# Self-loop scores of the edge attention: laid into each loaded score tile by VectorE instead of stored to the score matrix by GpSimd

## The chip, the cores and the metric

One Trainium2 chip, one core. The metric is the device time of one launch in microseconds (us), the median of several runs. The program is a whole two-layer graph network; the change touches one stage of it, the edge attention of layer 0.

## The reference, cut to what matters

The graph has 1250 nodes and 21250 directed edges. The attention adds one loop edge per node, computes a score for each edge and head, and takes a softmax over the edges that end at a node:

```python
loop = jnp.arange(n, dtype=edge_index.dtype)
src = jnp.concatenate([edge_index[0], loop])
dst = jnp.concatenate([edge_index[1], loop])
xl = (x @ Wl).reshape(n, H, D)
xr = (x @ Wr).reshape(n, H, D)
msg = xl[src] + xr[dst]
act = jnp.where(msg > 0, msg, NEG_SLOPE * msg)
e = jnp.einsum('ehd,hd->eh', act, att)
m = jax.ops.segment_max(e, dst, num_segments=n)
p = jnp.exp(e - m[dst])
denom = jax.ops.segment_sum(p, dst, num_segments=n)
alpha = p / (denom[dst] + 1e-16)
out = jax.ops.segment_sum(alpha[..., None] * xl[src], dst, num_segments=n)
out = out.reshape(n, HID)
return out @ W_up
```

H is 4 heads, HID is 256. An edge's score depends on its two nodes alone, so edges that occur several times share one score and differ only by a count.

## The kernel before, in words

**The score matrix.** The kernel keeps a dense matrix in device memory, `scores` (1250 x 1250 cells of 4 heads, f32, the head innermost). Every cell is first filled with -1e30 (`Fill`). GpSimd then writes the scores of the edges into their cells. The counts of the edges lie in a second matrix, `at`.

**Self-loop scores.** `front_phase` computes the score of each node with itself, tile by tile (10 tiles of 125 nodes), into the SBUF tile `loops` [125, 10, 4] (L387, L388). `Edges.diagonal` (L581) stores it to the diagonal of `scores` with eleven GpSimd DMAs (L587, L588), each counting on the semaphore `s_sc`.

**Edge scores.** `Edges` (L516) works through the edges in 84 batches of 2 x 128. For each batch GpSimd gathers rows of `xl` and `xr` (L572), VectorE scores them (`EdgeTurns.step`, L652 to L656), and GpSimd scatters the scores (L579). The order on GpSimd is written out in `Edges.gpsimd` (L597): gathers run five batches ahead, scatters start seven batches behind, and `diagonal` stands in front of the first scatter. A scatter waits for all earlier writes of `s_sc`, the eleven of the diagonal among them. These instructions run beside three stages in turn: the counting stage, the linear attention `mix0` and its output product `out0`. `FirstScores.load` (L632) waits until every score has landed and loads score tile 0 while `out0` still runs.

**The edge attention, `gat_phase` (L1065).** It starts when `out0` has ended, and goes over 10 tiles of 125 target nodes. A score tile is [125, 1250, 4] f32; three of them are held (`DEEP`), and SyncE loads tile t + 3 when tile t has been read. For tile t:
- VectorE takes the maximum per target and head. For tile 0 these are four reductions (`first_maxima`, L1178). For the others it is a tree: `halves` (L1186) folds the tile to one half in a buffer, and `maxima` (L1192, L1196) folds that on and reduces it.
- ScalarE takes the exponentials, head by head (L1284); TensorE transposes them (`spread`, L1340); VectorE multiplies them by the counts (`weigh`, L1217); TensorE multiplies by the node rows (`gather`, L1354).
- VectorE divides by the sum (`quotient`, L1234 to L1239), TensorE turns the result (L1363), ScalarE and VectorE split it into a high and a low part (L1288 and `rest`, L1244), and TensorE multiplies by `W_up` (`product`, L180 to L182).
- The result is added to the residual, normalized and scored for the experts (`GateTile`) one to three tiles later.

The orders are written out by hand, one loop per engine, and the engines meet at semaphores. VectorE's loop at step t has `weigh(t, 0)`, `quotient(t-1)`, `variance(t-2)`, `halves(t+1)`, `rest(t-1)`, `weigh(t, 1)`, `normal(t-2)`, `maxima(t+1)`, `weigh(t, 2)`, `weigh(t, 3)`. TensorE's has `gather(t, 0)`, a part of the expert scores, `spread(t, 2)`, `product(t-1, 0)`, 16 matmuls whose result nobody reads (`idle`, L1379), `gather(t, 1)`, `spread(t, 3)`, `product(t-1, 1)`, 10 more such matmuls, `gather(t, 2)`, `spread(t+1, 0)`, `gather(t, 3)`, `spread(t+1, 1)`, `turn_result(t)`. `Link` is a helper that makes VectorE wait for the end of its own last instruction; instructions without it follow each other with a small overlap.

Of the kernel before, what the change touches and what calls it, by code (L numbers as in the profile page):

```python
# [5 lines left out]
F32 = mybir.dt.float32  # L6
# [509 lines left out]
class Edges:  # L516
# [6 lines left out]
    def __init__(self, ph, src, dst, att, xl, xr, scores, loops, ring):  # L523
        self.src, self.dst, self.att, self.xl, self.xr = src, dst, att, xl, xr
        self.scores, self.loops, self.fill = scores, loops, None
# [48 lines left out]
    def scatter(self, pool, b, j):  # L574
        if j == 0:
            pool.wait_ge(self.s_e, b + 1)
        k = EB * b + j
        pool.wait_ge(self.s_sc, 16 * (T + 1) + 16 * k)
        pool.indirect_dma_start(self.scores, self.at(2, k), self.e[:, k, :], None).then_inc(self.s_sc, 16)  # L579

    def diagonal(self, pool):  # L581
        pool.wait_ge(self.fill.s_fill, self.fill.count)
        flat = self.scores.rearrange("s h -> (s h)")
        diag = flat[0:(N * N - 1) * HEADS].rearrange("(i x) -> i x", x=(N + 1) * HEADS)
        for t in range(T):
            n = min(R, N - 1 - t * R)
            pool.dma_start(diag[t * R:t * R + n, 0:HEADS], self.loops[0:n, t, :]).then_inc(self.s_sc, 16)  # L587
        pool.dma_start(self.scores[N * N - 1:N * N, :], self.loops[R - 1:R, T - 1, :]).then_inc(self.s_sc, 16)  # L588
# [5 lines left out]
    def landed(self, eng):  # L594
        eng.wait_ge(self.s_sc, 16 * (T + 1) + 16 * ET)

    def gpsimd(self, pool, first, end):  # L597
# [5 lines left out]
        for b in range(first, end):  # L603
            done = range(self.written(b - 1) if b else 0, self.written(b))
            if 0 in done:
                self.diagonal(pool)
# [458 lines left out]
def gat_phase(nc, first, scores, at, xl, ident, w_up, bias, part, dst, normed, gate_w, prob_out):  # L1065

    with Phase(nc, "gat") as ph:
# [7 lines left out]
        inv = ph.sb("inv", [R, 2, HEADS], F32)  # L1075
        res = ph.sb("res", [R, 2, HID], F32)
# [24 lines left out]
        with nc.Block(no_gpsimd_drain=True) as block:  # L1101
# [69 lines left out]
            def _(dve):  # L1171
                tree = Link(dve, s_tree)
                level = rows_x[:, :, :].rearrange("p t c -> p (t c)")[:, 0:N // 2 * HEADS].rearrange("p (s h) -> p s h", h=HEADS)

                def first_maxima():
                    dve.wait_ge(s_sc[0], LANDED)
                    for a in range(HEADS):
                        dve.tensor_reduce(top[:, 0, a:a + 1], sc[0][:, :, a], AX.X, ALU.max, negate=True).then_inc(s_top, 1)  # L1178

                def halves(t):  # L1180
# [3 lines left out]
                    if t == 1:  # L1184
                        dve.wait_ge(s_one, 1 + T)
                    tree(dve.tensor_tensor(level[:, :, :], sc[h][:, 0:N // 2, :], sc[h][:, N // 2:N, :], ALU.max))  # L1186
# [2673 lines left out]
def gps_kernel(nc, x, src, dst, rms_w, w_down, wl, wr, att, w_up, wq, bq, wk, bk, wv, bv, wo, bo,  # L3860
# [13 lines left out]
    with Phase(nc, "all") as keep:  # L3874
# [8 lines left out]
        with Phase(nc, "ffn0") as ffn0:  # L3883
            chosen = ffn0.sb("chosen", [CAPR, LIST, E_N], I32)
            share = ffn0.sb("share", [CAPR, LIST, E_N], F32)
            prob = ffn0.sb("prob", [R, T, E_N], F32)
            scored = Phase(nc, "scored")
            first = FirstScores(scored, scores)
            with Phase(nc, "layer0") as layer:
                act = activations(layer)  # L3890
                loops = layer.sb("loops", [R, T, HEADS], F32)
                with Phase(nc, "edge") as edge:
                    edges = Edges(edge, src, dst, att, xl, xr, scores, loops, first.ring)
# [85 lines left out]
```

## Time and profile before

| | us |
|---|---|
| median of 3 runs | 2928.65 |
| lowest and highest | 2922.87, 2935.39 |
| the profiled execution, its own time | 2933.26 |
| its span | 2931.5 |
| mean granted TensorE clock, share of full | 0.948 |

The span is the time from the first to the last instruction in the profile; the profiled execution's own time lies 1.8 us above it. Engines are written PE (TensorE), PEld (its weight loads), DVE (VectorE), ACT (ScalarE), POOL (GpSimd), SPq (SyncE's queue of DMAs).

### The profile page before, as it was taken

What the parts mean: (1) busy time and instruction counts of PE and PEld (TensorE: products, weight loads), DVE (VectorE), ACT (ScalarE), POOL (GpSimd) and SP (SyncE); (2) the same over time, 40 slices, a digit from 0 to 9 for tenths busy, and PEclk for the clock granted to TensorE, in tenths of its full rate; (3) what the DMA queues carried; (4) which work ended last, traced back from release to release, by engine and by line L of the source; (5) the groups of instructions that cost most, each with busy time, mean ns of one, the idle gap of its engine ahead of it and who ended that gap; (6) DMA issues with size and microseconds to landing.
All of it is one profiled execution on the core that took longest, in us unless ns stands there. A gap on an engine that the chain in (4) does not pass through costs nothing. (4 is left out here: it accounts for less than half of the span.)

```text
span 2931.5 us, 51143 instructions
## 1 busy us (share of the span) xinstructions
PE 2658.5 (91%) x19410; PEld 2503.5 (85%) x19410; DVE 1606.4 (55%) x3217; ACT 958.8 (33%) x1921; POOL 794.4 (27%) x772
## 2 busy tenths in 40 slices
PE   6677899999885998699979999899998999999788
PEld 6545899999885997588869999899998999999577
DVE  7777687777625886655553222354546332225755
ACT  4566433333203553244431010233334120001243
POOL 0567767667630342122200000000000001100054
PEclk9888999999995998799989999999999999999899
DMA  8834433433749873478753101111212653224382
GB/s 250 279 114 116 116 105 100 116 95 88 215 111 219 202 199 107 110 185 213 189 128 96 46 30 53 33 58 31 62 31 100 184 157 89 65 62 121 123 281 75
DMA packets 202067, 362.90 MB, mean 124 GB/s; under 512 B 33654, under 2 KB 135246, under 8 KB 200595
## 3 DMA queue, kind: packets, MB, share of 16 engines
q1 hardware_dynamic: 164193, 277.59, 32.3%
q0 software_dynamic: 36112, 80.96, 10.9%
q8 instruction: 150, 2.46, 0.4%
q10 hardware_dynamic: 1540, 1.30, 0.2%
q14 instruction: 72, 0.59, 0.1%
HBM read 272.97 MB, written 98.15 MB: 127 GB/s over the span
## 5 line engine op out<-in xcount | busy, mean ns | idle before, releaser
L180 PE MATMUL mix_bank<-sums_w_hi,layer_act_hi 128*125 128x256 f32 x1280 | 360.1, 281 | 0.0
L181 PE MATMUL mix_bank<-sums_w_lo,layer_act_hi 128*125 128x256 f32 x1280 | 359.2, 281 | 0.0
L182 PE MATMUL mix_bank<-sums_w_hi,layer_act_lo 128*125 128x256 f32 x1280 | 358.8, 280 | 0.0
L3195 POOL TENSOR_TENSOR sage_add<-sage_add,sage_bias 125x256 f32<-125x256 f32 x40 | 29.4, 736 | 1194.3 <-DMA sage_add<-resid 1194.3
L180 PEld LDWEIGHTS mix_bank<-sums_w_hi,layer_act_hi 128*125 128x125 f32 x1280 | 237.7, 186 | 0.8
L181 PEld LDWEIGHTS mix_bank<-sums_w_lo,layer_act_hi 128*125 128x125 f32 x1280 | 237.8, 186 | 0.2
L182 PEld LDWEIGHTS mix_bank<-sums_w_hi,layer_act_lo 128*125 128x125 f32 x1280 | 237.9, 186 | 0.0
L579 POOL DMA_INDIRECT scores<-edge_e,edge_idx x168 | 180.8, 1076 | 132.7 <-DMA scores<-edge_e,edge_idx 91.1
L572 POOL DMA_INDIRECT scored_ring<-xl,edge_idx x168 | 173.6, 1033 | 150.4 <-issue 129.5
L572 POOL DMA_INDIRECT scored_ring<-xr,edge_idx x168 | 170.8, 1017 | 51.5 <-issue 50.0
L929 PE MATMUL count_pa<-count_hot_s,count_hot_d 125*125 125x416 bf16 (+1 forms) x624 | 137.5, 383 | 26.5 <-DVE count_hot_s L839 24.6
L929 PEld LDWEIGHTS count_pa<-count_hot_s,count_hot_d 125*125 125x125 bf16 x624 | 94.0, 156 | 70.5 <-DVE count_hot_s L839 37.5
L180 PE MATMUL mix_bank<-layer_act_hi,mix_wq_hi 128*128 128x416 f32 (+1 forms) x384 | 137.5, 358 | 14.8 <-DVE mix_wq_lo L1612 14.7
L839 DVE TENSOR_SCALAR count_hot_s<-targets_node,targets_ends 125x1250 bf16<-125x1250 f16 x208 | 112.0, 574 | 53.9 <-issue 31.4
L182 PE MATMUL mix_bank<-layer_act_hi,mix_wq_lo 128*128 128x416 f32 (+1 forms) x384 | 136.1, 354 | 0.0
L181 PE MATMUL mix_bank<-layer_act_lo,mix_wq_hi 128*128 128x416 f32 (+1 forms) x384 | 135.7, 353 | 0.0
L1607 DVE SCALAR_TENSOR_TENSOR sums_y<-mix_bank,mix_ex 125x128 f32<-125x128 f32 (+2 forms) x104 | 37.3, 358 | 178.6 <-ACT mix_ex L1728 178.3
L3207 DVE TENSOR_TENSOR sage_z_lo<-sage_pz,sage_z_hi 125x256 fp32r<-125x256 f32 x80 | 33.9, 424 | 168.8 <-ACT sage_z_hi L3307 168.8
L1644 DVE RECIPROCAL sums_num<-sums_num 128x416 f32<-128x416 f32 (+1 forms) x42 | 115.8, 2758 | 19.0 <-ACT sums_num L1754 17.8
L1354 PE MATMUL gat_po<-gat_vals,gat_wgt 125*125 125x66 f32 x800 | 103.4, 290 | 15.2 <-DVE gat_wgt L1217 9.6
L1354 PEld LDWEIGHTS gat_po<-gat_vals,gat_wgt 125*125 125x125 f32 x800 | 100.7, 207 | 16.2 <-DVE gat_wgt L1217 10.2
L3267 DVE SCALAR_TENSOR_TENSOR sage_own<-sage_pagg,all_deg_inv,sage_own 125x256 f32<-125x256 f32 x70 | 33.8, 483 | 136.7 <-PE sage_pagg L3411 130.9
(630 smaller groups left out, 8554.9 us busy)
## 6 DMA issues: line engine op xcount, KB each, us to landing
ffn_raw<-in_L_ffn_w_dram SPq DMA_DIRECT2D x16, 2048.0 KB, 13.0
scores<-targets_hole SPq DMA_DIRECT2D x40, 546.9 KB
ffn_raw<-in_L_ffn_W_dram SPq DMA_DIRECT2D x16, 1024.0 KB
gat_sc<-scores SPq DMA_DIRECT2D x6, 2187.5 KB
lasting_raw<-in_L_mix_w_qkv_dram SPq DMA_DIRECT2D x24, 512.0 KB, 3.9
scored_ring<-scores SPq DMA_DIRECT2D x4, 2187.5 KB
layer_slab<-in_L_gnn_W_neigh_dram SPq DMA_DIRECT2D x7, 1024.0 KB
layer_slab<-in_L_gnn_W_self_dram SPq DMA_DIRECT2D x7, 1024.0 KB
```

Of the source, the lines that this page charges most:

```text
L180: pe.matmul(out, lhs[0], rhs[0], start=first, stop=False)
L181: pe.matmul(out, lhs[0], rhs[1], start=False, stop=False)
L182: return pe.matmul(out, lhs[1], rhs[0], start=False, stop=last)
L572: pool.indirect_dma_start(buf[:, slot, j, :], None, x, self.at(row, EB * b + j)).then_inc(self.s_g[slot], 16)
L579: pool.indirect_dma_start(self.scores, self.at(2, k), self.e[:, k, :], None).then_inc(self.s_sc, 16)
L839: dve.tensor_scalar(hot_s[:, j, :], node[:, :], ends[:, 0, j % 2, bass.ds(q, 1)], None, ALU.is_equal).then_inc(s_hot, 1)
L929: ins = pe.matmul(pa[:, c, 0:n], hot_d[:, j, :], hot_s[:, j, o:o + n], start=False, stop=False)
L1354: ins = pe.matmul(po[:, a * XW:(a + 1) * XW], wgt[:, a, b, :], vals[:, b, a, :], start=b == 0, stop=b == T - 1)
L1607: dve.scalar_tensor_tensor(y[0:p, U % 3, 0:n], from_, more, ex[0:p, U % 2, 0:n], ALU.add, ALU.max).then_inc(s_val, 1)
L1644: dve.reciprocal(num[:, o:o + n], num[:, o:o + n]).then_inc(s_rec, 1)
L3207: dve.tensor_tensor(z[1][:, u % T, :], pz[u % 4][:, 0:SLAB], z[0][:, u % T, :].bitcast(F32), ALU.subtract) \
L3267: dve.scalar_tensor_tensor(total, pagg[u % 2][:, 0:SLAB], deg_inv[:, t:t + 1], own[:, u % 2, :], ALU.mult, ALU.add).then_inc(s_tot, 1)
```

## The change

The eleven DMAs of `diagonal` are gone, and with them their share of the counts that the scatters and `landed` wait for. The first scatter waits for the filling instead. `loops` moves from the layer's buffers to a longer-lived set, so that `gat_phase` can read it. There, `own_edge(t, a)` lays the loop's score of head a into the 125 x 125 block of the loaded tile t that holds the diagonal: each cell becomes the larger of itself and `aside + loops`, where `aside` is 0 on the diagonal and -4e30 elsewhere. It is issued four times for a tile, in front of the four reductions for tile 0 and in front of the fold of `halves` for the others, and a `Link` stands behind the four. `aside` is made once, ahead of tile 0.

```diff
-        pool.wait_ge(self.s_sc, 16 * (T + 1) + 16 * k)
+        if k:
+            pool.wait_ge(self.s_sc, 16 * k)
+        else:
+            pool.wait_ge(self.fill.s_fill, self.fill.count)
         pool.indirect_dma_start(self.scores, self.at(2, k), self.e[:, k, :], None).then_inc(self.s_sc, 16)

-    def diagonal(self, pool):
-        pool.wait_ge(self.fill.s_fill, self.fill.count)
-        flat = self.scores.rearrange("s h -> (s h)")
-        diag = flat[0:(N * N - 1) * HEADS].rearrange("(i x) -> i x", x=(N + 1) * HEADS)
-        for t in range(T):
-            n = min(R, N - 1 - t * R)
-            pool.dma_start(diag[t * R:t * R + n, 0:HEADS], self.loops[0:n, t, :]).then_inc(self.s_sc, 16)
-        pool.dma_start(self.scores[N * N - 1:N * N, :], self.loops[R - 1:R, T - 1, :]).then_inc(self.s_sc, 16)
...
-        eng.wait_ge(self.s_sc, 16 * (T + 1) + 16 * ET)
+        eng.wait_ge(self.s_sc, 16 * ET)
...
-            if 0 in done:
-                self.diagonal(pool)
...
+        aside = ph.sb("aside", [R, R], F32)
...
+                def own_edge(t, a):
+
+                    cells = sc[t % DEEP][:, t * R:(t + 1) * R, a]
+                    return dve.scalar_tensor_tensor(cells, aside[:, :], loops[:, t, a:a + 1], cells, ALU.add, ALU.max)
+
                 def first_maxima():
+                    tree(dve.tensor_scalar(aside[:, :], ident[0:R, 0:R], -1.0, -4.0 * NEG, ALU.add, ALU.mult))
                     dve.wait_ge(s_sc[0], LANDED)
+                    for a in range(HEADS):
+                        ins = own_edge(0, a)
+                    tree(ins)
                     for a in range(HEADS):
                         dve.tensor_reduce(top[:, 0, a:a + 1], sc[0][:, :, a], AX.X, ALU.max, negate=True).then_inc(s_top, 1)
...
                     if t == 1:
                         dve.wait_ge(s_one, 1 + T)
+                    for a in range(HEADS):
+                        ins = own_edge(t, a)
+                    tree(ins)
                     tree(dve.tensor_tensor(level[:, :, :], sc[h][:, 0:N // 2, :], sc[h][:, N // 2:N, :], ALU.max))
```

## Rows read from the trace of the kernel before

**Rows 1.** The page: busy time and share of the span of each engine.
```profile
PE 2658.5 (91%) x19410; PEld 2503.5 (85%) x19410; DVE 1606.4 (55%) x3217; ACT 958.8 (33%) x1921; POOL 794.4 (27%) x772
```
**Rows 2.** Stretches: start:end, length, PE, PEld, DVE, ACT, POOL, PEclk, DMA share, GB/s.
```profile
1009.00:1031.00 22.00, 21.86 (x187) 21.04 (x186) 19.20 (x39) 12.66 (x12) 8.41 (x4) 1.00 0.85 214
```
**Rows 3.** Order of time on POOL: start, duration, instruction, [idle before it <- releaser].
```profile
162.84 5.61 POOL L587 DMA_DIRECT2D scores<-layer_loops  x10
...
172.80 1.23 POOL L572 DMA_INDIRECT scored_ring<-xl,edge_idx  x1 [3.85 <-DVE edge_e L656]
```
**Rows 4.** Order of time where the output product ends and the attention begins.
```profile
871.40 0.97 POOL L579 DMA_INDIRECT scores<-edge_e,edge_idx  x1 [2.31 <-DMA scores<-edge_e,edge_idx]
...
881.47 0.84 SPq L38 DMA_DIRECT2D part<-out_res  x2
...
890.37 9.20 DVE L1178 TENSOR_REDUCE gat_top<-scored_ring 125x1 f32<-125x1250 f32 x4 [8.92 <-PEq L98]
```
**Rows 5.** Order of time in the attention's first three tiles.
```profile
905.77 4.47 PE L1354 MATMUL gat_po<-gat_vals,gat_wgt 125*125 125x66 f32 x20 [5.59 <-POOL gat_vals L1156]
...
917.58 2.76 DVE L1186 TENSOR_TENSOR gat_rows_x<-gat_sc 125x2500 f32<-125x2500 f32 x1 [16.19 <-DMA gat_sc<-scores]
...
922.02 4.47 PE L1354 MATMUL gat_po<-gat_vals,gat_wgt 125*125 125x66 f32 x20 [9.59 <-DVE gat_wgt L1217]
...
943.52 0.42 DVE L1244 TENSOR_TENSOR gat_gat_lo<-gat_pr,gat_gat_hi 128x250 fp32r<-128x250 f32 x1
...
948.09 0.77 PE L180 MATMUL gat_pr<-gat_up_hi,gat_gat_hi 128*125 128x512 f32 x1
```
**Rows 6.** Order of time on PE and DVE in the steady part of the attention.
```profile
969.72 0.50 PE L180 MATMUL gat_pr<-gat_up_hi,gat_gat_hi 128*125 128x512 f32 x1 [0.44 <-DVE gat_gat_lo L1244]
...
1009.05 2.75 DVE L1186 TENSOR_TENSOR gat_rows_x<-gat_sc 125x2500 f32<-125x2500 f32 x1
...
1026.24 2.38 PE L1354 MATMUL gat_po<-gat_vals,gat_wgt 125*125 125x66 f32 x20
...
1028.65 0.23 DVE L1062 TENSOR_REDUCE ffn_prob<-gat_po 125x8 f32<-125x64 f32 x1 [0.56 <-PE gat_po L1354]
...
1030.93 0.15 DVE L1002 TENSOR_SCALAR gat_var<-gat_mv 125x1 f32<-125x1 f32 x1
1031.00 2.75 DVE L1186 TENSOR_TENSOR gat_rows_x<-scored_ring 125x2500 f32<-125x2500 f32 x1
...
1033.79 0.42 DVE L1244 TENSOR_TENSOR gat_gat_lo<-gat_pr,gat_gat_hi 128x250 fp32r<-128x250 f32 x1
...
1034.26 0.50 PE L180 MATMUL gat_pr<-gat_up_hi,gat_gat_hi 128*125 128x512 f32 x1
```
**Rows 7.** Single lines: duration in ns least/median/greatest, first and last start, shapes.
```profile
L1203 DVE TENSOR_TENSOR gat_cnt<-gat_cnt,all_ident x10: 288/290/1647, 899.5 to 1107.7; 125x125 f32<-125x125 f32 x10
L728 DVE TENSOR_REDUCE targets_lim<-targets_rows x1: 409/409/409, 48.4 to 48.4; 85x1 f32<-85x250 f32 x1
L2575 DVE SCALAR_TENSOR_TENSOR choose_within<-choose_far,choose_place x1: 514/514/514, 1195.0 to 1195.0; 125x80 f16<-125x80 f32 x1
L2595 DVE TENSOR_TENSOR ffn_share<-ffn_share,choose_said x1: 204/204/204, 1208.6 to 1208.6; 104x24 f32<-104x24 f32 x1
```
**Rows 8.** Order of time on PE near the attention's end: an instruction behind a pause.
```profile
1138.69 0.43 PE L1363 MATMUL gat_pr<-all_ident,gat_res 125*128 125x125 f32 x2 [1.27 <-DVE gat_res L1239]
```
**Rows 9.** Stretches with or behind three pauses (columns as in rows 2).
```profile
780.00:782.00 2.00, 2.00 (x20) 1.90 (x18) 1.90 (x5) 0.00 (x0) 1.63 (x2) 1.00 0.85 325
...
1138.00:1144.00 6.00, 5.16 (x22) 4.03 (x23) 3.73 (x14) 1.74 (x5) 0.90 (x2) 0.72 0.24 72
...
2004.00:2006.00 2.00, 2.00 (x12) 1.96 (x12) 1.41 (x4) 1.83 (x4) 0.00 (x0) 1.00 0.84 235
```
**Rows 10.** PE's pauses elsewhere, order of time; the last stands for four alike.
```profile
778.61 0.35 PE L180 MATMUL out_bank<-out_w_hi,layer_act_hi 128*125 128x256 f32 x1 [2.17 <-DVE out_res L2114]
...
2003.17 0.43 PE L180 MATMUL mix_bank<-layer_act_hi,mix_wq_hi 128*128 128x418 f32 x1 [1.18 <-DVE mix_wq_lo L1612]
```

More of the change, by code:

```diff
@@ L516, with __init__ @@
 class Edges:
-    def __init__(self, ph, src, dst, att, xl, xr, scores, loops, ring):
+    def __init__(self, ph, src, dst, att, xl, xr, scores, ring):
         self.src, self.dst, self.att, self.xl, self.xr = src, dst, att, xl, xr
-        self.scores, self.loops, self.fill = scores, loops, None
+        self.scores, self.fill = scores, None
         self.idx = ph.sb("idx", [P, 3, ET], I32)
@@ L1062, in keep, with gat_phase @@
         dve.tensor_reduce(self.prob[:, n, :], every, AX.X, ALU.add).then_inc(self.s_prob, 1)
-def gat_phase(nc, first, scores, at, xl, ident, w_up, bias, part, dst, normed, gate_w, prob_out):
+def gat_phase(nc, first, scores, loops, at, xl, ident, w_up, bias, part, dst, normed, gate_w, prob_out):
     with Phase(nc, "gat") as ph:
@@ L3886, in gps_kernel @@
             prob = ffn0.sb("prob", [R, T, E_N], F32)
+            loops = ffn0.sb("loops", [R, T, HEADS], F32)
             scored = Phase(nc, "scored")
@@ L3890, in gps_kernel @@
                 act = activations(layer)
-                loops = layer.sb("loops", [R, T, HEADS], F32)
                 with Phase(nc, "edge") as edge:
-                    edges = Edges(edge, src, dst, att, xl, xr, scores, loops, first.ring)
+                    edges = Edges(edge, src, dst, att, xl, xr, scores, first.ring)
                     begun = MixStart(edge, wq, wk, wv)
@@ L3913, in gps_kernel @@
                     run.__exit__(None, None, None)
-            gat_phase(nc, first, scores, at, xl, ident, w_up, bo, part, xs[0], y[0], gate0_w, prob)
+            gat_phase(nc, first, scores, loops, at, xl, ident, w_up, bo, part, xs[0], y[0], gate0_w, prob)
             ffn0.takes(scored)
```

## The prediction

> **What bounds the kernel now.** I read the page first. Over the whole launch TensorE is busy 91% of the span and VectorE 55% [rows 1], but the change touches only two places, so I read those stage by stage. The stretches come next. In the steady part of the attention TensorE is busy 21.86 of 22 us and VectorE 19.20, at full clock [rows 2]. 21.95 us is also the period of a tile: the fold of one tile starts at 1009.05 and the next at 1031.00 [rows 6]. So TensorE looks like the bound and VectorE seems to have 2.8 us to spare in each tile. That reading has to be tested in the order of time, because part of TensorE's work are the 26 unread matmuls, and because a full engine can still be released by another one.
>
> The order of time of both engines over one period shows the following loop [rows 6]. TensorE's `gather(t, 3)` runs from 1026.24 to 1028.62. VectorE waits for it (idle 0.56 us) and starts the next stretch at 1028.65: quotient, statistics and variance to 1031.08, the fold 1031.00 to 1033.75, `rest` 1033.79 to 1034.21. TensorE's `product` starts at 1034.26, 0.05 us after `rest` has ended. From there TensorE works without a pause to the end of its next `gather(t, 3)`. The loop is closed: 5.6 us on VectorE, then 16.4 us on TensorE, which is the whole period. Inside VectorE's 5.6 us nothing is idle, and TensorE fills that time with work that ends just as `rest` does. Three tiles earlier TensorE even waited 0.44 us for `rest` [rows 6]. So both engines bound the loop at this point, and the fold lies in VectorE's part. The chain of waits on the page follows only the last 3% of the span and says nothing about this stage.
>
> **The part that is removed.** GpSimd issues eleven DMAs for the diagonal, ten of them in 5.61 us from 162.84, and then sits idle for another 3.85 us until VectorE's edge scores release the next gather at 172.80 [rows 3]. Without the eleven it reaches the same wait some 6 us earlier and leaves it at the same time. Gain: 0. The first scatter's new wait, for the filling, costs nothing either, since the diagonal stood behind the same wait and started with no idle time [rows 3]. The later scatters and `landed` only lose eleven counts that were in long before. Even if GpSimd did run earlier, its last scatter is issued at 871.40, while the output product's last store is issued at 881.47 and the attention starts at 890.37, released by the barrier behind TensorE's queue and not by the score tile [rows 4]. 10 us of cover stand between GpSimd and the end of that stage. The 1250 small writes that go were moved when the DMA engines had room. Bounds of this part: 0 to -6 us; I take 0.
>
> **The part that is added: one own_edge.** It is a VectorE instruction on 125 x 125 f32 from SBUF. The nearest unstrided row is the addition of the identity to the counts, same size: 290 ns [rows 7]. But here the cells lie 16 bytes apart, since the head is innermost, for the operand that is read and for the result. What such a step costs is seen in the reductions. The first maxima reduce 1250 cells 16 bytes apart, 9.20 us for four, 2.30 us each [rows 4]; an unstrided reduction of 250 takes 409 ns, of which 250 x 1.04 are elements if they go at the rate of the fold (2.75 us less a start of 0.15, over 2500 elements) [rows 6, 7]. So unstrided 1.04 ns for an element, strided (2300 - 150) / 1250 = 1.72 ns. An addition that reads and writes f32 at 20 to 32 bytes takes 204 ns for 24 elements [rows 7], and less a start of 150 to 160 that is 1.8 to 2.2 ns. Both agree on about 1.9, so one own_edge is 0.155 + 125 x 1.9 = 0.39 us. Lower bound: 0.29. Upper bound: the instruction with f16 results 20 bytes apart, 514 ns for 80 elements or 4.5 ns for each [rows 7], which would make it 0.72 us; I take 0.39, since the f32 row is nearer in type.
>
> The Trainium skill has a rule that speaks against this change (SBUF — State Buffer, the note on cachelines in "Door 1: The DMA port swizzle"): full rate needs at least two accesses in a 16-byte line, and each step to a new line is charged. Every cell here is in a line of its own. This trace agrees, 1.72 against 1.04 ns. By the page on VectorE alone (VectorE: DVE Perf Modes, "Mode 1× (REGULAR) — the baseline"), one element in a cycle whatever the stride, own_edge would stay at 0.29 us, and the sum below would be 8 x 0.96 = 7.7 instead of 10.9 us.
>
> **Four of them and the Link.** Instructions without a Link overlap: the variance ends at 1031.08, the fold has started at 1031.00, so 0.08 us [rows 6]. The four take 4 x (0.39 - 0.08) = 1.24 us. Behind the fourth stands a Link, so the fold, which overlapped the instruction ahead of it by 0.08 before, now starts some 0.04 us after it (as `rest` does after the linked fold, 1033.75 to 1033.79 [rows 6]): 0.12 us more. Sum for a tile: 1.36 us (bounds 4 x 0.21 + 0.12 = 0.96 and 4 x 0.64 + 0.12 = 2.7).
>
> **Which tiles pay.** The folds are those of tiles 1 to 9.
> - Tile 0 (the first maxima, plus `aside`, about 1.7 us): hidden. Its first `weigh` is ready about 901.4, and TensorE starts `gather(0, 0)` at 905.77, released by GpSimd's copy of the rows [rows 5]. VectorE then idles 16.19 us for score tile 1 [rows 5]. If that cover were gone it would cost 1.7 us.
> - Tile 1: pays. The fold starts when the tile lands, 917.58, and the `weigh` behind it releases TensorE at 922.02 [rows 5].
> - Tile 2: hidden. `rest` ends at 943.94, the product it feeds starts at 948.09 because TensorE, at half clock, comes from other work [rows 5]; 4.1 us of cover.
> - Tiles 3 to 9, seven of them: pay in full, by the loop above. VectorE's idle time in a period, the 0.56 us [rows 6] among it, lies outside the 5.6 us, where it waits for TensorE's own work, and shifts with that.
>
> That is 8 x 1.36 = 10.9 us.
>
> **What the new pause may do to the clock.** TensorE will pause 1.36 us in front of `product` in each of seven tiles. Near the attention's end it paused 1.27 us [rows 8], and over the 6 us from 1138 its granted clock was 0.72 of the full 2.4 GHz on average, a part of it at the lower level of 1.2 GHz [rows 9]: 6 x 0.28 = 1.7 us of work lost. But a pause of 2.17 us in the output product and four of 1.18 us in the second `mix` [rows 10] left the clock at 1.00 (the first and one of the four stand in [rows 9]). One pause of six lost the clock, so I charge 7 x 1/6 x 1.7 = 2.0 us (bounds 0 and 12).
>
> **Sum.** 10.9 + 2.0 = 12.9 us. The profiled execution took 2933.26 us (span 2931.5), so 2946.2 us for its like; it lay 4.6 us above the median of the runs, and against that median of 2928.65 I forecast 2941.6 us.
>
> **The rivals.**
> - *VectorE's slack takes it.* It has 2.8 us idle in a period [rows 2] and the change adds 1.36. Then only tile 1 pays, and the time is 2928.65 + 1.4 = 2930, not slower in any measurable way. Against it: the 0.05 us between `rest` and `product` [rows 6]. It would hold if TensorE came to `product` later than `rest` ends by more than 1.36 us.
> - *GpSimd's relief reaches the end.* If the whole chain of scatters moves up by 6 us and the stage's barrier with it, the time is 2928.65 - 6 + 12.9 = 2935.5, and with the slack taking the rest 2924. Against it: the idle 3.85 us and the 10 us of cover [rows 3, 4]. It decides only if the attention's start waits for `landed`.
> - *The clock falls at every pause.* 10.9 + 7 x 1.7 = 22.8 us, 2951.5. For it: the only pause of this length in this very stage did it [rows 8, 9].
> - *Strided writes are dear.* 0.72 us for one own_edge, 2.7 for a tile, 8 x 2.7 = 21.6 plus 2: 2952. For it: one row, of another type [rows 7].
>
> **How the numbers follow.** The forecast has 0.62, the clock rival 0.14, the dear writes 0.10, the slack 0.08, GpSimd's relief 0.04, and 0.02 is left for what I don't see. I take 0.5%, 14.6 us, as what a measurement of this kernel can tell from no change, its own runs spreading over 12.5 us. The forecast's own range is 7.7 to 16 us, so about a fifth of its 0.62 is over the bound; with both dear rivals, slower by over 0.5% gets 0.37. Faster by over 0.5% needs a mechanism that I see only in the two combined: 0.04. The rest, 0.59, is within. The range reaches from below the slack's case to above both dear ones, less the outer tenths: 2929 to 2957.
>
> **What would show it.** In the changed profile: four instructions of own_edge for each tile with 0.39 us each; the fold starting 1.4 us later behind the variance; TensorE's L180 behind a pause of some 1.3 us released by `rest` (L1244) from tile 3 on; a period of 23.3 us against 21.95; GpSimd idle about 10 us in front of the gather at 172.80, and the attention starting at 890 as before. The forecast is wrong if the period stays near 22 us, if the clock falls in the middle of the attention (a period over 24.5), or if the start at 890.37 moves.

## The result and the profile after

| | before | after |
|---|---|---|
| median, us (15 runs each, beside each other) | 2926.27 | 2942.53 |
| lowest and highest | 2922.8, 2937.18 | 2934.51, 2953.0 |
| the profiled execution, its own time | 2933.26 | 2949.02 |
| its span | 2931.5 | 2946.9 |
| mean granted clock, share of full | 0.948 | 0.948 |

The ratio is 1.0052 with a 95% interval of 1.0040 to 1.0064, or 15.2 us (11.7 to 18.7) on 2926.27. The change makes the kernel slower, by an amount that lies across the bound of 0.5%. The ratio compares all runs of both kernels; the two medians by themselves lie 16.3 us apart. The forecast of 2941.6 us was 0.9 us off, and part of that closeness is luck: it started from the median of the first three runs, 2928.65, which lay 2.4 us above the median of the fifteen, and its sum of 12.9 us was 2.3 us below the 15.2. The sum lies in the interval, near the lower end.

The page's busy time by engine, after (before: [rows 1]):

```profile
PE 2658.4 (90%) x19410; PEld 2502.0 (85%) x19410; DVE 1622.9 (55%) x3258; ACT 959.3 (33%) x1921; POOL 770.4 (26%) x761
```

VectorE has 41 instructions more (40 own_edge and one `aside`) and is busy 16.5 us longer. GpSimd has the eleven DMAs less and is busy 24.0 us less. Those two sums say little about the time: GpSimd's relief is the larger and brings nothing, VectorE's load is spread over 55% of the span and yet is the whole loss.

The order of time in the steady part of the attention, on all engines, around the place of the change; to be laid beside [rows 6]:

```profile
1037.43 0.15 DVE L994 TENSOR_SCALAR gat_var<-gat_mv 125x1 f32<-125x1 f32 x1
1037.50 1.50 DVE L1171 SCALAR_TENSOR_TENSOR scored_ring<-gat_aside,ffn_loops,scored_ring 125x125 f32<-125x125 f32 x4
...
1039.04 2.76 DVE L1191 TENSOR_TENSOR gat_rows_x<-scored_ring 125x2500 f32<-125x2500 f32 x1
...
1040.59 0.38 PE L1020 MATMUL gat_pt<-all_ident,gat_y 125*128 125x125 f32 x2
1041.84 0.42 DVE L1249 TENSOR_TENSOR gat_gat_lo<-gat_pr,gat_gat_hi 128x250 fp32r<-128x250 f32 x1
...
1042.31 0.50 PE L180 MATMUL gat_pr<-gat_up_hi,gat_gat_hi 128*125 128x512 f32 x1 [1.34 <-DVE gat_gat_lo L1249]
...
1058.65 0.23 DVE L1054 TENSOR_REDUCE ffn_prob<-gat_po 125x8 f32<-125x64 f32 x1 [0.56 <-PE gat_po L1359]
...
1060.93 0.15 DVE L994 TENSOR_SCALAR gat_var<-gat_mv 125x1 f32<-125x1 f32 x1
1061.00 1.51 DVE L1171 SCALAR_TENSOR_TENSOR gat_sc<-gat_aside,ffn_loops,gat_sc 125x125 f32<-125x125 f32 x4
...
1062.55 2.76 DVE L1191 TENSOR_TENSOR gat_rows_x<-gat_sc 125x2500 f32<-125x2500 f32 x1
```

Read it from the top. The variance starts at 1037.43, own_edge where the fold used to start, 0.07 us later. The fold follows after 1.54 us, `rest` (L1249) right behind it, and TensorE's `product` (L180) 0.05 us behind `rest`, now with a pause of 1.34 us. TensorE's work after that takes as long as before, and VectorE waits for it with the same 0.56 us. From fold to fold it is 1062.55 - 1039.04 = 23.51 us, where it was 21.95. The loop is the same, with 1.56 us more in its VectorE part.

What TensorE waited for in the whole attention, total, times, longest: the kernel after, then the kernel before.

```profile
PE gat_pt L1345 <- ACT gat_prob L1289: 16.0, 1, 16.0
PE gat_pr L180 <- DVE gat_gat_lo L1249: 11.3, 9, 2.0
PE gat_po L1359 <- DVE gat_wgt L1222: 11.0, 2, 10.2
```

```profile
PE gat_pt L1340 <- ACT gat_prob L1284: 14.3, 1, 14.3
...
PE gat_pr L180 <- DVE gat_gat_lo L1244: 0.4, 1, 0.4
```

The second line is the change: 0.4 us in one wait have become 11.3 in nine.

Stretches of the two kernels (columns as in [rows 2]); after: the whole attention, its steady part, and the two places in its loop where the clock fell; before: the same first two.

```profile
895.00:1173.70 278.70, 238.67 (x1814) 226.14 (x1814) 214.37 (x422) 130.02 (x112) 62.70 (x53) 0.88 0.67 170
970.00:1109.00 139.00, 129.96 (x1072) 124.00 (x1072) 121.36 (x248) 72.93 (x63) 36.10 (x24) 0.99 0.75 189
1104.00:1120.00 16.00, 14.52 (x110) 13.45 (x109) 14.97 (x31) 6.26 (x6) 3.37 (x3) 0.89 0.17 53
...
972.00:976.00 4.00, 4.00 (x20) 3.73 (x19) 3.89 (x7) 0.60 (x1) 1.36 (x1) 0.63 0.75 107
```

```profile
890.00:1159.00 269.00, 241.04 (x1814) 230.11 (x1814) 197.52 (x381) 130.03 (x112) 78.51 (x52) 0.87 0.71 176
965.00:1096.00 131.00, 129.63 (x1091) 124.32 (x1089) 114.91 (x229) 75.52 (x64) 50.11 (x24) 1.00 0.83 209
```

Where the time of this pair of profiles went: the attention starts at 895.02 instead of 890.37 (4.65 us), lasts 278.7 instead of 268.7 us (10.0), and what follows is 0.8 us longer. Within the 10.0: up to the fold of tile 3 the kernel after is 2.8 us quicker, because its clock came back earlier (0.72 of full in the stretch from 920 to 960, against 0.61); from the fold of tile 3 to that of tile 9 it takes 141.2 instead of 130.4 us; from there to the end 64.2 instead of 62.2, and that holds the lapse of the third line above, 16 x 0.11 = 1.8 us. The other lapse, 4 x 0.37 = 1.5 us, lies in the six periods: 6 x 1.56 + 1.5 = 10.9 of the 10.8 us. One pair of profiles doesn't settle the first terms, which are larger than what is asked; the experiments do.

### The profile page after: what moved, and what is told of

Same layout as the page of the kernel before. It is cut to its first block and busy times, and to the rows that moved or that the text cites. A ratio compares the mean times of both kernels' runs of the same rounds, so it can differ in the third digit from the quotient of the medians.

```text
span 2946.9 us, 51174 instructions
## 1 busy us (share of the span) xinstructions
PE 2658.4 (90%) x19410; PEld 2502.0 (85%) x19410; DVE 1622.9 (55%) x3258; ACT 959.3 (33%) x1921; POOL 770.4 (26%) x761
## 5 line engine op out<-in xcount | busy, mean ns | idle before, releaser
L180 PE MATMUL mix_bank<-sums_w_hi,layer_act_hi 128*125 128x256 f32 x1280 | 360.0, 281 | 0.0
L180 PEld LDWEIGHTS mix_bank<-sums_w_hi,layer_act_hi 128*125 128x125 f32 x1280 | 237.6, 186 | 1.0
L180 PE MATMUL mix_bank<-layer_act_hi,mix_wq_hi 128*128 128x416 f32 (+1 forms) x384 | 137.0, 357 | 15.0 <-DVE mix_wq_lo L1617 15.0
L180 PE MATMUL out_bank<-sums_w_hi,layer_act_hi 128*125 128x256 f32 x320 | 96.4, 301 | 15.7 <-DVE sums_w_lo L2080 9.1
L1359 PEld LDWEIGHTS gat_po<-gat_vals,gat_wgt 125*125 125x125 f32 x800 | 97.4, 201 | 15.4 <-DVE gat_wgt L1222 11.5
```

The source lines that it names most:

```text
L180: pe.matmul(out, lhs[0], rhs[0], start=first, stop=False)
L1359: ins = pe.matmul(po[:, a * XW:(a + 1) * XW], wgt[:, a, b, :], vals[:, b, a, :], start=b == 0, stop=b == T - 1)
```

## The experiments

My theory: own_edge lengthens the one loop that binds both engines, in eight or nine tiles, and nothing else of the change matters. Rivals: the buffers that moved (`loops` among the longer-lived ones, `aside` new); GpSimd's relief, as a gain that hides a larger loss; the clock. A number for each comes with the kernel before run on the same chip beside it.

**e1_both: own_edge, and the diagonal still stored as before.**

```diff
 (kernel after)
+        pool.wait_ge(self.s_sc, 16 * (T + 1) + 16 * k)
...
+            if 0 in done:
+                self.diagonal(pool)
```

> The changed kernel with GpSimd's eleven DMAs of the diagonal put back (their counts and waits too), so own_edge alone is added to the kernel before. Theory (all of the cost is own_edge in the loop of rest and product, the removed DMAs were free): as slow as the changed kernel, 12 to 17 us over the kernel before, period of a tile 23.5 us. Rival (some 5 us of the loss come from the removal or from what it shifts ahead of the attention, since in the two profiles the attention starts 4.65 us later and lasts only 10.0 us longer): about 10 us over the kernel before.

Measured: 2939.26 us, ratio 1.0055 (1.0036 to 1.0074), so 16.1 us. The attention takes 278.5 us and a period 23.53. With the stores back, the time is that of the kernel after: the whole loss is own_edge's. The same nine pauses stand in front of `product`, the one of 2.01 us at 962.68 among them, and behind that one the period lasted 26.99 us (959.41 to 986.40) where the kernel after took 23.69 at the same place.

**e2_neither: neither own_edge nor the diagonal's stores.** The self loops' scores still reach the tiles, as edges: the graph's edge list ends with one loop for each node, 1250 of its 21250 edges. So on this graph the stores and own_edge both bring a score that the edges bring anyway.

```diff
 (kernel after)
-                    for a in range(HEADS):
-                        ins = own_edge(t, a)
-                    tree(ins)
... (the same for tile 0, and the making of aside)
```

> The changed kernel without own_edge and without making aside, and without the DMAs of the diagonal: the loops' scores reach the score matrix only as edges of the list. Theory: the removal is free and brings nothing, 0 +- 2 us against the kernel before, period 21.95 us. Rival (the removal or the moved buffer costs): +5 us, with the attention starting some 5 us later. Second rival (the 6 us of GpSimd's work were worth something): -3 to -6 us.

Measured: 2931.27 us beside 2924.45 before, ratio 1.0009 (0.9996 to 1.0023). The two medians lie further apart than the ratio, which takes in all runs. The period is 21.95 us again. The relief of GpSimd brings nothing that can be measured. GpSimd's order of time in e2_neither, against [rows 3]:

```profile
164.88 1.09 POOL L572 DMA_INDIRECT scored_ring<-xr,edge_idx  x1 [0.30 <-issue]
170.97 1.16 POOL L572 DMA_INDIRECT scored_ring<-xl,edge_idx  x1 [4.99 <-DVE edge_e L648]
```

No DMA stands between the gathers any more, and GpSimd waits 4.99 us for the same releaser, VectorE's edge scores (5.00 us in the kernel after, 5.37 to 8.07 in the other six profiles without the stores), where I had expected 10. With the stores the wait of 3.85 us in [rows 3] isn't the rule. It stands in the kernel before and in e3_layout, and in the other four profiles with the stores there is none, as in e1_both:

```profile
167.15 5.66 POOL L587 DMA_DIRECT2D scores<-ffn_loops  x10
...
173.61 1.02 POOL L572 DMA_INDIRECT scored_ring<-xl,edge_idx  x1 [0.30 <-issue]
```

From the end of the gather ahead to the start of this one it takes 6.4 to 6.7 us in those four and 10.0 to 10.1 in the two, and 5.0 to 8.1 us without the stores. So in some executions the stores themselves hold the gather up, by some 1.4 us if the shortest of each kind are set side by side. The gather starts at 170.97 here, at 175.00 in the kernel after, and with the stores at 172.80 in the kernel before and 173.61 in e1_both: no order by whether there are stores. The same is seen at the end of the whole chain, where the attention starts: at 889.7 on average over the six profiles with the stores (886.5 to 894.7), at 889.9 over the eight without them (885.2 to 895.0). What stands between the last scatter and that start is less than the 10 us of the prediction, but enough: SyncE's queue carries the load of score tile 0, which waits for the last scatter, ahead of the last store of `out0`. In the kernel before it has issued that load by 874.31 and then waits until 881.47 for VectorE's `out_res`, 7.2 us; in the kernel after 7.1.

**e3_layout and f2_layout_again: the kernel before, with only the buffers of the change.**

```diff
 (kernel before)
-                loops = layer.sb("loops", [R, T, HEADS], F32)
+            loops = ffn0.sb("loops", [R, T, HEADS], F32)
...
+        aside = ph.sb("aside", [R, R], F32)
```

> The kernel before with only the buffers of the change: loops allocated in the longer-lived set, aside allocated and unused. Theory: 0 +- 2 us. Rival (the shifted addresses cost the missing 5 us): +5 us.

Measured: 2928.72 us, ratio 1.0010 (0.9999 to 1.0020). Since the interval only just reached 1, I ran it again in a later batch.

> The kernel before with only the moved and the added buffer, a second time. Theory (the buffers cost nothing, the +0.1% of its first time was chance): a ratio within 0.1% of 1, so that the two times together hold 1. Rival: +0.1% again.

Measured: 2927.37 us, ratio 0.9985 (0.9969 to 1.0001). The two together: nothing. They also show what one profile is worth. It is the same kernel twice, and its attention started at 889.97 and 894.65 and took 267.2 and 256.0 us, the granted clock from 920 to 960 being 0.63 in one and 0.86 in the other. Over the four profiles without own_edge (before, e2_neither and these two) the attention takes 263.5 us on average (256.0 to 268.7), over the two with it (after, e1_both) 278.6. That is 15.1 us apart, and the start at 895.02, the latest of all fourteen profiles, lies 0.4 us behind that of f2_layout_again, so it falls within what chance does.

**e4_slack: own_edge of tiles 2 to 9 moved out of the loop's VectorE part**, two steps ahead, in front of `weigh(t, 3)`.

```diff
 (kernel after; in halves own_edge stays for tile 1 alone)
...
 (VectorE's step t)
+                    if t + 2 < T:
+                        dve.wait_ge(s_sc[(t + 2) % DEEP], LANDED * ((t + 2) // DEEP + 1))
+                        for a in range(HEADS):
+                            ins = own_edge(t + 2, a)
+                        tree(ins)
                     weigh(t, 3)
```

> The changed kernel with own_edge of tiles 2 to 9 moved in VectorE's order to the place ahead of weigh(t, 3) two tiles earlier, where VectorE idles 1.75 us for TensorE's transposes; the work is the same. Theory (what costs is the place in the loop, not the work): the seven payments vanish, period back to 21.95 to 22.1 us, 1 to 4 us over the kernel before. Rival (VectorE as a whole is the bound, or strided accesses slow the other engines): still 10 us or more over it.

Measured: 2939.31 us, ratio 1.0048 (1.0034 to 1.0061). That is 14.0 us. As to the time, the expectation failed: I gave it 1 to 4 us and it kept nearly all of the loss. In the trace half of it came true. Where nothing disturbs it the period is 21.96 us again (991.73 to 1013.69, and the last two). But `weigh(t, 3)` now stands behind own_edge, and TensorE's `gather(t, 3)` needs it. In order of time on PE, e4_slack:

```profile
1032.02 2.78 PE L1365 MATMUL gat_po<-gat_vals,gat_wgt 125*125 125x66 f32 x20 [0.99 <-DVE gat_wgt L1223]
1034.60 2.41 PE L1351 MATMUL gat_pt<-all_ident,gat_prob 125*125 125x125 f32 x10
```

After a pause of 0.99 us the ten matmuls of `spread` take 2.41 us, where they take 1.30 at full clock. That period lasted 23.50 us and the next 22.79. And the waits of VectorE in this stage, e4_slack (first line: 16.2 of it is tile 1's, which the kernel after has too, with 13.3):

```profile
DVE gat_sc L1171 <- DMA gat_sc<-scores: 21.3, 2, 16.2
```

So the new wait for the tile's landing cost 5.1 us once, early. In this profile the stage is 9.0 us longer than before: 3.3 ahead of tile 1's fold, 5.3 between the folds of tiles 1 and 9, 0.4 behind. Where the rest of the 14 us lies, one profile doesn't show. VectorE's 2.8 us of slack in a period [rows 2] are real, but they are in pieces in front of instructions that TensorE waits for.

**e5_rest_first: `rest` ahead of own_edge and the fold.**

```diff
 (kernel after, VectorE's step t)
+                    if 1 <= t <= T:
+                        rest(t - 1)
                     if t + 1 < T:
                         halves(t + 1)
-                    if 1 <= t <= T:
-                        rest(t - 1)
```

> The changed kernel with rest(t-1) moved ahead of own_edge and the fold in VectorE's order; nothing else. Theory (the loop is closed by rest): product no longer waits for rest, and own_edge shows up only at the next meeting point, gather(t, 2), which had some 0.7 us to spare behind weigh(t, 2): period some 22.8 us instead of 23.5, total 5 to 9 us over the kernel before. Rival (the cost is VectorE's work as such): no change against the changed kernel, +12 to 17 us.

Measured: 2945.27 us, ratio 1.0052 (1.0032 to 1.0073). The pause in front of `product` is gone, and the periods at full clock are 22.95 us, as expected (22.8). The total, 15.2 us over the kernel before, gave nothing of that back; 5 to 9 was expected. In order of time on PE, e5_rest_first:

```profile
1048.41 1.31 PE L1384 MATMUL gat_po<-gat_up_hi,gat_gat_hi 128*125 128x184 f32 x10
1050.53 2.40 PE L1359 MATMUL gat_po<-gat_vals,gat_wgt 125*125 125x66 f32 x20 [0.81 <-DVE gat_wgt L1222]
1052.77 2.31 PE L1345 MATMUL gat_pt<-all_ident,gat_prob 125*125 125x125 f32 x10
...
1055.99 4.44 PE L1359 MATMUL gat_po<-gat_vals,gat_wgt 125*125 125x66 f32 x20
```

The pause has moved to `gather(t, 2)`, 0.81 us, and at this one the clock fell: 2.31 us for `spread` and 4.44 for the gather that takes 2.3 at full clock. This period lasted 27.52 us and the next 24.59. Of the six pauses of 0.80 to 0.83 us at this place, one for a tile, three were followed by half clock (1050.53, 1078.05 and 1125.60) and three were not. Over the 170 us from 966 the mean clock was 0.94, by estimate 10 us of full-clock time, where the kernel before kept 1.00 from 965 to 1096. In this profile the clock takes more than the shorter period gives. It is of one of the slower runs (2950.38 us), so how large that part is in the median stays open.

**e6_double: own_edge of tiles 1 to 9 issued twice.**

```diff
 (kernel after, halves)
-                    for a in range(HEADS):
-                        ins = own_edge(t, a)
-                    tree(ins)
+                    for _ in range(2):
+                        for a in range(HEADS):
+                            ins = own_edge(t, a)
+                        tree(ins)
```

> The changed kernel with own_edge of tiles 1 to 9 issued twice (a Link between, the result is the same). Theory: each tile pays its 1.55 us again, period 25.1 us, 8 x 1.56 = 12.5 us over the changed kernel, 25 to 31 us over the kernel before, perhaps more where the longer pause of TensorE lets the clock fall. Rival (the first own_edge pays for something that happens once): less than 8 us over the changed kernel.

Measured: 2988.58 us, ratio 1.0198 (1.0161 to 1.0235), 58 us over the kernel before. From the fold of tile 3 on no period ran wholly at full clock. The quickest, 972.81 to 998.02, had a mean clock of 0.93 and took 25.21 us. The kernel after took 23.69 at the same place (968.33 to 992.02), with a lapse of its clock in it too, so the second set cost 1.52 us there, as the sum has it. The later ones took 26.4 to 32.6. In e6_double, one `product` in order of time, and the stretch of the steady part:

```profile
1065.46 0.79 PE L180 MATMUL gat_pr<-gat_up_hi,gat_gat_hi 128*125 128x512 f32 x1 [2.89 <-DVE gat_gat_lo L1250]
1066.05 0.63 PE L181 MATMUL gat_pr<-gat_up_lo,gat_gat_hi 128*125 128x512 f32 x1
```

```profile
966.00:1146.00 180.00, 160.97 (x1140) 152.40 (x1139) 138.28 (x291) 78.40 (x66) 37.08 (x25) 0.85 0.63 155
```

A mean clock of 0.85 over 180 us is 27 us of full-clock time lost. By this estimate the instructions added account for about 27 of the 58 us (9 tiles by twice 1.5), the clock for most of the rest. The cost of own_edge is in proportion only as long as the pause in front of `product` stays short.

**e7_packed: one instruction in a row in place of four with a step.** It leaves out the loops' scores in `loops`, as the block is compared with a constant; the tiles have them from the edge list.

```diff
 (kernel after)
-                    cells = sc[t % DEEP][:, t * R:(t + 1) * R, a]
-                    return dve.scalar_tensor_tensor(cells, aside[:, :], loops[:, t, a:a + 1], cells, ALU.add, ALU.max)
+                    cells = sc[t % DEEP][:, t * R:(t + 1) * R, :]
+                    return dve.tensor_tensor(cells, aside[:, :, :], cells, ALU.max)
... (issued once for a tile; aside is [R, R, HEADS] and filled with -4e30)
```

> The changed kernel with the four strided own_edges of a tile replaced by one tensor_tensor over the same 125 x 500 f32 cells in a row, against a buffer of -4e30: the loops' scores are left out of it (they are in the list of edges). Theory (the stride and the four starts make the price): one instruction of 0.67 us, 0.75 us for a tile with the Link, period 22.7, total 6 to 9 us over the kernel before. Rival (the price is that of the cells touched, stride or not): 125 x 500 at the strided rate, period 23.3 or more, no gain against the changed kernel.

Measured: 2933.31 us, ratio 1.0026 (1.0005 to 1.0046), 7.6 us. The line of the instruction in e7_packed, and the two of own_edge in the kernel after (duration in ns least/median/greatest, first and last start):

```profile
L1171 DVE TENSOR_TENSOR gat_sc<-gat_aside,gat_sc x6: 667/670/680, 913.8 to 1069.6; 125x500 f32<-125x500 f32 x6
```

```profile
L1171 DVE SCALAR_TENSOR_TENSOR gat_sc<-gat_aside,ffn_loops,gat_sc x24: 433/443/452, 921.2 to 1085.6; 125x125 f32<-125x125 f32 x24
L1171 DVE SCALAR_TENSOR_TENSOR scored_ring<-gat_aside,ffn_loops,scored_ring x16: 431/439/448, 895.3 to 1109.1; 125x125 f32<-125x125 f32 x16
```

The same 500 cells take 0.67 us in a row and 1.50 us in four strided pieces. The period is 22.67 us, 0.72 over 21.95: the period follows the loop's VectorE part here too, at half the amount. The total's interval still touches that of the kernel after (1.0046 and 1.0040), so it is the period that shows it.

**e9_rest_fill12 and f3_rest_fill12_again: the kernel before with `rest` first and less filler on TensorE.**

```diff
 (kernel before; rest ahead of the fold as in e5_rest_first)
-                        idle(16)
+                        idle(12)
...
-                        idle(10)
+                        idle(7)
```

> The kernel before (diagonal stored by GpSimd) with rest(t-1) ahead of the fold and 12 and 7 unread matmuls instead of 16 and 10 in each tile of the attention. Theory: with rest first TensorE is the bound of the loop, and 7 x 0.115 = 0.8 us of its filler can go until weigh(t, 2) becomes the bound: period 21.2 us, 4 to 6 us under the kernel before. Rival (VectorE's 5.6 us still close the loop elsewhere, or the clock falls in the shorter filler): 0, or slower.

Measured: 2930.49 us, ratio 1.0006 (0.9985 to 1.0028), with a period of 21.40 us, 0.55 under the kernel before. The loop did get shorter; the total doesn't show it. Again:

> The kernel before with rest(t-1) ahead of the fold and 12 and 7 unread matmuls instead of 16 and 10, a second time: its attention was 5.7 us shorter in the profile, its ratio 1.0006 with an interval of 0.2% either way. Theory (the attention's gain is real and the rest of the runs' spread is chance): a ratio of 0.998 to 0.9985. Rival (the gain is given back where the clock falls): 1.000 or more.

Measured: 2927.23 us, ratio 0.9984 (0.9967 to 1.0000), period 21.39. f2_layout_again, which does nothing, got 0.9985 in the same batch, so I don't call it a gain. 7 x 0.55 = 3.9 us is 0.13%, which lies in both intervals: these runs neither show it nor rule it out.

**f1_packed_rest: the whole computation, arranged by what the others showed.** GpSimd, with time to spare here, builds the block `aside + loops` of 125 x 500 in a row, VectorE lays it in with one instruction, and `rest` comes first.

```diff
 (kernel after; rest first as in e5_rest_first)
-                    cells = sc[t % DEEP][:, t * R:(t + 1) * R, a]
-                    return dve.scalar_tensor_tensor(cells, aside[:, :], loops[:, t, a:a + 1], cells, ALU.add, ALU.max)
+                    cells = sc[t % DEEP][:, t * R:(t + 1) * R, :]
+                    dve.wait_ge(s_diag, t + 1)
+                    tree(dve.tensor_tensor(cells, diag[:, t % 2, :, :], cells, ALU.max))
...
+                    pool.tensor_tensor(diag[:, t % 2, :, :], aside[:, :].unsqueeze(2).to_broadcast([R, R, HEADS]),
+                                       loops[:, t, :].unsqueeze(1).to_broadcast([R, R, HEADS]), ALU.add).then_inc(s_diag, 1)
... (its semaphores and buffers, and its places in GpSimd's order)
```

> The changed kernel with both remedies, its whole computation kept: GpSimd, which idles 13 us in a tile, adds aside and the loops' scores into a 125 x 500 buffer in a row, VectorE lays it with one instruction, and rest(t-1) goes ahead of it and of the fold. Theory: 0.75 us for a tile, of which gather(t, 2) has 0.7 us to spare, so the period is back at 22.0 and TensorE does not pause; 1 to 4 us over the kernel before. Rival (the two savings don't add, or GpSimd's addition holds VectorE up): a period of 22.7 or more, 6 us or more over it.

Measured: 2933.52 us beside 2930.35 before, ratio 1.0005 (0.9991 to 1.0018). The order of time in f1_packed_rest on all engines, and its steady stretch:

```profile
1019.21 1.02 POOL L1150 TENSOR_TENSOR scored_ring<-scored_ring,ffn_loops 125x500 f32<-125x500 f32 x1
...
1021.85 0.41 DVE L1261 TENSOR_TENSOR gat_gat_lo<-gat_pr,gat_gat_hi 128x250 fp32r<-128x250 f32 x1
...
1022.18 0.67 DVE L1186 TENSOR_TENSOR scored_ring<-scored_ring 125x500 f32<-125x500 f32 x1
1022.88 2.76 DVE L1203 TENSOR_TENSOR gat_rows_x<-scored_ring 125x2500 f32<-125x2500 f32 x1
...
1025.07 0.48 PE L180 MATMUL gat_pr<-gat_up_hi,gat_gat_hi 128*125 128x512 f32 x1
```

```profile
962.00:1094.00 132.00, 130.27 (x1092) 124.69 (x1091) 118.46 (x233) 73.59 (x64) 40.67 (x30) 1.00 0.80 197
```

`rest` ends 2.8 us ahead of the `product` that it releases, TensorE doesn't pause, the clock holds at 1.00 and the period is 22.11 us, 0.16 over the kernel before. No loss is left that these runs can tell from none. A gain over the kernel before isn't shown.

**f4_filler_moved: twelve of the sixteen filler matmuls ahead of `product` instead of behind it.**

```diff
 (kernel after, TensorE's step t)
+                    if 1 <= t < T:
+                        pe.wait_ge(s_hi, t)
+                        idle(12)
...
-                        idle(16)
+                        idle(4)
```

> The changed kernel with 12 of the 16 unread matmuls moved in front of product, where TensorE pauses 1.34 us for rest; their number is the same, VectorE's order too. Theory (own_edge costs by the loop through rest, and on top by the pauses that let the clock fall): TensorE reaches gather(t, 2) earlier and is held there by weigh(t, 2), period 22.8 at full clock, with a pause of some 0.7 us; 6 to 9 us over the kernel before, so 6 to 9 under the changed one. Rival (moving the filler only moves the wait): no gain.

Measured: 2935.89 us, ratio 1.0030 (1.0012 to 1.0047), 8.8 us. The period is 22.97 us. In order of time in f4_filler_moved:

```profile
1032.23 1.53 PE L1384 MATMUL gat_po<-gat_up_hi,gat_gat_hi 128*125 128x184 f32 x12
1033.34 0.42 DVE L1249 TENSOR_TENSOR gat_gat_lo<-gat_pr,gat_gat_hi 128x250 fp32r<-128x250 f32 x1
...
1033.82 0.50 PE L180 MATMUL gat_pr<-gat_up_hi,gat_gat_hi 128*125 128x512 f32 x1
```

The twelve fill the pause, and there are twelve fewer behind `product`. Without touching VectorE this gives back some 6 of the 15 us, if the two ratios are set side by side; their intervals overlap (up to 1.0047, from 1.0040), so the period, 0.54 us shorter, is the better witness. In place of the pause TensorE now waits for `weigh`, 15.6 us in nine waits, against 11.0 in two.

## Why the prediction was right

- *The removed part costs and brings 0.* Right as to the time (e1_both, e2_neither), but not for the reason given first. It was to leave its wait for VectorE's edge scores "at the same time" with or without the stores. In four of the six profiles with the stores there was no such wait behind them, and without them it was 5.0 to 8.1 us and not about 10. What holds is the second reason, the cover at the end of `out0`, though it is 7.2 us and not 10.
- *The loop through `rest` and `product` closes the period, so VectorE's slack doesn't take it.* Right. TensorE's L180 waits for L1249 in nine waits, 1.34 to 1.36 us each in six of them, and the period follows every change of the VectorE part: 21.95 without, 22.67 with 0.67 us, 23.51 with 1.50, and 1.52 more again with twice that (25.21 against 23.69). That refutes the rival of the slack, and e4_slack shows what the slack is worth in practice.
- *One own_edge 0.39 us, 1.36 for a tile.* A little small. It takes 0.44 us, follows the one before by 0.355, and the tile pays 1.55. Over eight tiles that is 12.4 instead of 10.9 us. The estimate of 1.9 ns for a strided element should have been (443 - 155) / 125 = 2.3. The rival of dear writes, at 4.5 ns, was far off; whether its row was slow for its f16 results or for something else, no run here separates.
- *Tile 0 hidden, tile 1 pays.* Right. TensorE's `gather(0, 0)` still waited for GpSimd's copy, 3.6 us, and started 15.2 us into the attention, as before (15.4). From the first instruction on tile 1 to its gather it takes 5.97 us (921.16 to 927.13) where it took 4.44, so 1.53 more.
- *Tile 2 hidden.* It was not. The `product` behind its fold waited 0.97 us in the profile after, and as long in e1_both:

```profile
949.97 0.50 PE L180 MATMUL gat_pr<-gat_up_hi,gat_gat_hi 128*125 128x512 f32 x1 [0.97 <-DVE gat_gat_lo L1249]
```

  The 4.1 us of cover rested on TensorE being at half clock (0.50 until 950, 0.81 from 950 to 954), and in this execution the clock was back at 0.96 from 942 to 946. A cover that rests on the clock is a matter of chance: in e3_layout and f2_layout_again, one kernel, the clock from 920 to 960 was 0.63 and 0.86, and `rest` ended 4.1 and 0.4 us ahead of this `product`. The prediction should have charged tile 2 with a part of its 1.36 us.
- *Clock: one pause in six, 2.0 us.* Three of the nine pauses of the profile after were followed by half clock. One, of 0.30 us at 1154.33, stands behind another of 1.27 us, where the kernel before lost its clock too [rows 8, 9], so it adds nothing. The others are the one of 2.00 us at 971.60 (1.5 us lost, by the stretch from 972 to 976) and the one of 1.34 us at 1112.84 (1.8 us; the matmuls behind it take 0.63 us where they take 0.39). That is 3.3 us, so the term was too small by 1.3, inside its bounds. In e1_both only the pause of 2.01 us was followed by half clock, but for longer: that period was 4.8 us over the 22.21 that the 20.65 of this period without own_edge and 1.56 make. A charge of 1.7 us for a lapse is an average of what varies. The rival in which every pause costs 1.7 us is refuted by five pauses of 1.34 to 1.36 us with periods of 23.5 between them. In e6_double, with pauses of 2.5 to 3.6 us, it came near.
- *The start at 890.37 stays.* It moved to 895.02, which I had named as a sign against me. e3_layout and f2_layout_again, one kernel, differ by as much. Since e1_both has the whole loss and e2_neither none of it, a second cause isn't needed; the sign was badly chosen, as one profile can't tell so much.

The sum with the measured sizes: 8 x 1.55 for tiles 1 and 3 to 9, up to 1.5 for tile 2, and 3.3 for the clock, so 15.7 to 17.2 us, against 15.2 measured (11.7 to 18.7). The mechanism was right; the terms left small were the price of own_edge (10.9 for 12.4), tile 2 (0 for about 1) and the clock (2.0 for 3.3). I put more on "within 0.5%" than on "slower"; the ratio's interval, 1.0040 to 1.0064, lies on both sides of it.

## What to carry to other kernels

Whether an engine's idle time can take an instruction is read in the order of time, at the place where it will stand. Here VectorE was idle 2.8 us in a period and TensorE was "full", and still every added microsecond ahead of `rest` was paid in each tile, for TensorE's fullness was partly filler and `rest` released it with 0.05 us to spare. If something must be added to such a loop, put the instruction that releases the other engine first, and lay the added data in a row: the two together took the 15 us to nothing that could be measured, where the order alone gave nothing back (e5_rest_first, 15.2 us) and the row alone about half (e7_packed, 7.6 us). And before paying for a piece of work, see whether its result is there already: here the edge list had the loops, and e2_neither, without either form, took no longer than the kernel before that could be measured. A graph whose list lacks them needs one of the two. Moving the addition to "where there is slack" only moved the wait.

## What the hardware showed that I had not expected

- *A short pause may cost more than itself.* At full clock, pauses of 0.81 us (e5_rest_first) and 0.99 us (e4_slack) were followed by matmuls at half clock for some microseconds, and the period was 4.6 us longer (27.52 against 22.95) and 1.5 us longer (23.50 against 21.96), while three other pauses of 0.80 to 0.81 us in e5_rest_first and five of 1.34 to 1.36 us in the kernel after were not. The pause of 2.00 us cost 1.5 us in the kernel after and that of 2.01 us 4.8 us in e1_both. With pauses of about 0.5 us in each tile the clock stayed at 1.00 (e7_packed from 960 to 1100, f4_filler_moved from 972 to 1126). In e6_double, pauses of 2.54 to 3.58 us took the mean clock to 0.85. What decides in the single case stays open.
- *The price of a step of 16 bytes for a VectorE instruction with two tiles read and one written:* 2.3 ns for a cell, against (670 - 155) / 500 = 1.03 ns in a row.
- *A GpSimd instruction of one column takes its length from what VectorE does beside it.* The power of the variance, in order of time in the kernel before, after, e7_packed and f1_packed_rest:

```profile
1031.16 3.00 POOL L992 TENSOR_TENSOR gat_half<-gat_var,gat_power 125x1 f32<-125x1 f32 x1 [3.32 <-DVE gat_var L1002]
```

```profile
1037.66 0.69 POOL L984 TENSOR_TENSOR gat_half<-gat_var,gat_power 125x1 f32<-125x1 f32 x1 [3.32 <-DVE gat_var L994]
```

```profile
1024.26 0.67 DVE L1171 TENSOR_TENSOR scored_ring<-gat_aside,scored_ring 125x500 f32<-125x500 f32 x1
...
1024.42 0.91 POOL L984 TENSOR_TENSOR gat_half<-gat_var,gat_power 125x1 f32<-125x1 f32 x1 [3.31 <-DVE gat_var L994]
```

```profile
1022.01 0.55 POOL L984 TENSOR_TENSOR gat_half<-gat_var,gat_power 125x1 f32<-125x1 f32 x1 [1.78 <-DVE gat_var L994]
```

  In the first three it ends 0.40 to 0.41 us behind the end of the VectorE instruction beside which it started: the fold (1033.75, then 1034.16), the first of the four own_edge (1037.94, then 1038.35), the packed one (1024.93, then 1025.33). All three read two tiles in SBUF. Beside `rest`, which reads one of its two from PSUM, it takes 0.55 us, here and in a tile of the kernel before that has no fold beside it (1118.99). That the number of SBUF tiles decides is my guess; no run changes it alone. Some 16 of the 24 us by which GpSimd is less busy after the change are this (78.5 to 62.7 us in the attention), and not the DMAs that were removed. It cost nothing here, since what needs the power comes later.
